# GpSimd's normalised rows ahead of its sums of the chosen in groups 7 and 8, and two uses of PSUM banks 5 and 7 exchanged, in an attention and mixture-of-experts layer

## What is computed

```python
x = x + xattn(layernorm(x), ctx)      # q = xn @ Wq.T; k, v = split(ctx @ Wkv_expand.T)
xf = layernorm(x)                     # softmax(q k / sqrt(32), causal) @ v @ Wout.T
probs = softmax(xf @ gate_w.T); top_p, top_i = top_k(probs, 2)
y = sum of top_p * (silu(xf @ fc1_e) * (xf @ fc2_e)) @ proj_e over the two experts
y = y + sigmoid(xf @ shared_gate_w.T) * ((silu(xf @ s_fc1) * (xf @ s_fc2)) @ s_proj)
x = x + y
```

## Time and profile before

| what | value |
|---|---|
| three runs, median (lowest to highest) | 1514.23 us (1508.57 to 1515.4) |
| the profiled execution: its time, and its span | 1513.03 us, 1511.3 us |
| busy: TensorE, its weight loads | 98%, 83% of the span |
| busy: VectorE, ScalarE, GpSimd | 59%, 43%, 41% |
| mean granted clock of TensorE | 0.99 of full |
| chain that ended last: TensorE, ScalarE, VectorE | 91%, 4%, 2% |

### The profile page before, as it was taken

One profiled execution on the slowest core, in us unless ns is written; L12 is line 12 of the kernel. 1 busy time (PEld: TensorE's weight loads), 2 busy tenths in 40 slices (PEclk: granted clock), 3 DMA queues, 4 the chain that ended last, 5 costly groups with the idle time before them and its releaser, 6 DMA issues.

```text
span 1511.3 us, 28047 instructions
## 1 busy us (share of the span) xinstructions
PE 1477.5 (98%) x9928; PEld 1256.4 (83%) x9928; DVE 894.0 (59%) x1453; ACT 653.0 (43%) x1833; POOL 617.5 (41%) x513
## 2 busy tenths in 40 slices
PE   7999999999789999999999999999999999999999
PEld 7888888887568899999999999887888888888887
DVE  6778888887555587876877867455223232233322
ACT  6999999998653323323323323332112121111211
POOL 3344566666343387685865864102101102011010
PEclk9999999999799999999999999999999999999999
DMA  6243445443155588867877765462303022030210
GB/s 232 80 118 117 124 114 133 125 120 93 52 132 117 155 324 323 270 254 262 284 249 267 267 221 179 167 216 86 97 15 112 28 69 63 8 111 28 64 48 28
DMA packets 102903, 217.42 MB, mean 144 GB/s; under 512 B 43696, under 2 KB 48816, under 8 KB 98064
## 3 DMA queue, kind: packets, MB, share of 16 engines
q1 hardware_dynamic: 91184, 184.71, 37.5%
q0 software_dynamic: 11616, 31.35, 7.1%
HBM read 168.86 MB, written 47.17 MB: 143 GB/s over the span
## 4 chain that ended last, share of the span: by engine, by line
PE 91%; ACT 4%; DVE 2%; DMA 1%; issue 1%; POOL 1%; POOLq 0%; SPq 0%; DVEq 0%; ACTq 0%
PE psum L827 64%; PE psum L1145 11%; PE psum L960 4%; ACT probs L1258 3%; PE psum L951 2%; PE psum L910 2%; PE psum L1047 2%; PE psum L982 2%; PE psum L1071 1%; PE psum L1012 1%; PE psum L969 1%; PE psum L941 1%; ACT probsT L1239 0%; DMA wkv_raw<-in_wkv 0%; POOL xn L1475 0%
## 5 line engine op out<-in xcount | busy, mean ns | idle before, releaser
L1582 POOL DMA_INDIRECT routed<-expert_out_dram,slot_b x56 | 56.8, 1014 | 478.0 <-DVE slot_b L2043 327.5
L2061 DVE TENSOR_TENSOR h_s<-psum,silu_s 128x512 f32<-128x512 f32 x66 | 45.6, 691 | 298.5 <-PE psum L827 298.5
L1258 ACT ACTIVATE probs<-psum,minus_max,rs 112x112 f32<-112x112 f32 x512 | 220.5, 482 | 2.2 <-DVE minus_max L1713 2.0
L827 PE MATMUL psum<-nT_hi,ws_hi 128*128 128x512 f32 x528 | 208.8, 395 | 3.1 <-DVE nT_lo L1984 2.8
L827 PE MATMUL psum<-nT_lo,ws_hi 128*128 128x512 f32 x528 | 208.6, 395 | 0.0
L827 PE MATMUL psum<-nT_hi,ws_lo 128*128 128x512 f32 x528 | 208.6, 395 | 0.0
L1554 POOL DMA_INDIRECT xg<-normed_dram,tile_ids x63 | 150.4, 2388 | 35.7 <-DMA tile_ids<-lists_dram 12.8
L827 PE MATMUL psum<-wj_hi,gT_hi 128*128 128x352 f32 x504 | 162.8, 323 | 0.0
L827 PE MATMUL psum<-wj_hi,gT_lo 128*128 128x352 f32 x504 | 162.3, 322 | 0.0
L827 PE MATMUL psum<-wj_lo,gT_hi 128*128 128x352 f32 x504 | 161.8, 321 | 0.0
L1372 ACT ACTIVATE silu_s<-psum 128x512 f32<-128x512 f32 x66 | 39.5, 598 | 241.3 <-PE psum L827 241.3
(11 more groups left out here) (252 smaller groups left out, 3534.2 us busy)
## 6 DMA issues: line engine op xcount, KB each, us to landing
wj_raw<-in_w_experts SPq DMA_DIRECT2D x35, 1408.0 KB, 6.6
wj_raw<-in_w_experts SPq DMA_DIRECT2D x35, 768.0 KB, 5.9
wj_raw<-in_w_shared SPq DMA_DIRECT2D x22, 768.0 KB, 5.8
expert_out_dram<-y_c SPq DMA_DIRECT2D x63, 256.0 KB, 3.2
base<-x_dram SPq DMA_DIRECT2D x8, 1024.0 KB, 5.8
xT_raw<-in_xT SPq DMA_DIRECT2D x32, 224.0 KB, 4.7
x_in<-in_x SPq DMA_DIRECT2D x32, 224.0 KB, 4.3
x_res<-in_x SPq DMA_DIRECT2D x32, 224.0 KB, 3.0
```

Source lines behind the costliest of these rows:

```text
L827: mm = pe.matmul(out_ap, u, v, start=(n == 0), stop=(n == last))
L1258: done = act.activation(probs[:, j % 2, 4 * r + m, :], psum[0:SEQ, r, m * SEQ:(m + 1) * SEQ], ACT.Exp, bias=minus_max[:, r, m:m + 1], scal ...
L1582: pool.indirect_dma_start(out=routed[:, b % 2, c, :], out_offset=None, in_=expert_out_dram, in_offset=bass.IndirectOffsetOnAxis(ap=slot_b[ ...
L2061: dve.tensor_tensor(h_s[:, :], bank(b), silu_s[:, :], ALU.mult).then_inc(emptied_b[b], 1)
```

## The change

Two parts. In GpSimd's loop `rows(t - 3)` is moved ahead of `sum_chosen(g - 1)`. Both run in one step only in (7, 2), for batch 27, and in (8, 2), for batch 31. In `TURNS` the rows' transposes (`normT`, groups 0 to 7) take bank 7 and the outputs (`outT`) bank 5. At the start of `hidden0` the wait on bank 5's last shares becomes one on bank 7's. No instruction is added or removed.

```diff
@@ TURNS
     TURNS += [((_j, "probsT", k), 1, (7, 5, 4, 6)[k]) for k in range(4)]
-    TURNS += [((_j, "normT", 0), "norm", 5), ((_j, "outT", 0), 1, 7),
+    TURNS += [((_j, "normT", 0), "norm", 7), ((_j, "outT", 0), 1, 5),
               *([((_j, "rank", 0), "rank", 7)] if _j == 2 else []),
@@ TensorE, hidden0
                     pe.wait_ge(S["n0_split"], KC)
-                    wait_emptied(pe, NG, 0, "probsT", 1)
+                    wait_emptied(pe, NG, 0, "probsT", 0)
                     wait_emptied(pe, NG, 0, "outT")
@@ GpSimd, body
+                    if there(g, j, 3) and t - 3 >= FROM:
+                        rows(t - 3)
                     if j == 2 and routes(g):
                         sum_chosen(g - 1)
-                    if there(g, j, 3) and t - 3 >= FROM:
-                        rows(t - 3)
```

## The result

| | median (lowest to highest), runs | profiled execution: span |
|---|---|---|
| before | 1510.79 us (1508.57 to 1515.4), 5 | 1511.3 us |
| after | 1501.68 us (1499.46 to 1502.69), 5 | 1499.9 us |

The ratio is 0.993, with a 95% interval of 0.9912 to 0.9947: the change makes the kernel about 9 us faster (0.7%). The forecast was 1505.9 us, its range ended at 1501.8.

A forecast was written before the change was run, and what follows sets the result against it. TensorE was taken to bound the kernel, busy 90% or more of nearly every slice. Terms -9.25 - 0.5 + 2.0 = -7.75 us, from a base of 1513.6, gave 1505.9 us; range 1501.8 to 1510.2.

The forecast's parts named there:

- Rows ahead of the sums, step 7.2: Group 7, j = 2: TensorE's 6.93 us wait for batch 27's rows goes and the clock recovers; gain 9.25 us.
- The sums are not late: Step 7.2: sums behind the rows still run at 394.5 to 396.25, before `ranks` needs them; cost nothing.
- Step 8.2: Group 8, j = 2: batch 31's rows, ready 0.48 us after TensorE asks, come early; gain 0.5 us.
- Bank 7 for the rows' transposes: Rows' transposes wait for ScalarE's first copy of shares instead of the second; gain 0.
- Bank 5 for the outputs: Queries now wait for VectorE's `aT_lo`, late at j = 0 of groups 3 to 6; 2.0 us lost.
- The collision: Step 7.2: GpSimd's rows pass overlaps VectorE's second multiplication of shares, making it 0.47 us longer; TensorE loses nothing.
- The rivals: Four alternatives: queries never wait (0.16), another wait takes part (0.16), it does not do what it says (0.04), slower (0.04).
- The queries never wait: Rival, chance 0.16: VectorE's lateness in the four steps is made up; -9.75 us, 1503.9 us.
- Slower: Rival, chance 0.04: queries' wait for `aT_lo` spreads from 4 steps to all 27; at 0.75 us each +10.5, 1524.1 us.

The follow-up runs named there:

- the order alone: Only GpSimd's order changed (rows ahead of the sums) against the kernel before, banks as before: 1502.04 us, ratio 0.9932.
- the best of both: Kernel before with GpSimd's new order and the shares' first two quarters exchanged (bank 5, then 7), queries behind the rows' transposes: 1498.69 us, 0.9911.
- the square: Times of 25 steps: before 306.00 us; shares' first two quarters exchanged 302.53; `normT`/`outT` banks exchanged 305.41; both exchanges 307.86.

## Why the prediction was right or wrong

- **Rows ahead of the sums, step 7.2: right.** -9.25 us predicted, -9.66 measured in this pair of executions and -9.0 on the mean of ten traces. The idle time alone (6.93) would have missed 2 to 2.7 us. They came back with the clock, as I said: TensorE's stretch from the rows' transposes to `x1` took 2.84 us less. "All three steps are set by ScalarE's exponentials" was wrong for 7.2 before, which was set by the slow projection and by VectorE behind it. That the measure was good to 0.4 us is in part luck, as a step there takes 11.9 or 13.1 us by the clock of the execution. The predicted length, 13 to 13.5 us, was reached by the order alone (13.15) and the best of both (13.01); the other three have 12.62 to 12.84. The granted clock was to be above 0.8: it is 0.87 from 388 to 401 us after.
- **The sums are not late: right.** They end at 394.33, 2 us before the ranks ask.
- **Step 8.2: right.** -0.5 us predicted. The wait went, and from the rows' transposes of 8.1 to those of 8.2 it is 9.55 us after and 10.18 before, 0.63 less. That the whole rest of the span also came out at -0.5 us says little: it takes between 1085.4 and 1087.9 us in the ten traces.
- **Bank 7 for the rows' transposes: the step that failed.** "In rows 3 they follow the shares' transposes without a gap, so there is nothing to gain: 0." They gained 0.17 us in each of some 25 steps, 2.5 to 3.5 us in all. The chain and the matmul row have no gap because the shares' last matmuls were still draining; the gap was in the weight loads. The term had no bound either: an earlier release was priced at exactly nothing. With it the exchange of banks gained 0.6 to 1.0 us where it was to lose 2.0.
- **Bank 5 for the outputs: right in mechanism, and in its sum by luck.** 2.0 us predicted as four waits of 0.5. Measured were three waits that cost 0.3 each (0.9 us) and two stops of 1.5 us together that I had not seen coming; 1.9 to 2.9 us by the square. A wait of 0.15 us cost 0.3. The upper bound had added "some 0.2 us to start again", which no row before showed; 0.15 is what the runs show.
- **The collision: right.** GpSimd's rows started 0.17 us before VectorE's multiplication, which is the order in which a lock would bite. The timeline of VectorE after:

```profile
386.91 1.53 DVE L1700 TENSOR_TENSOR probs<-probs,rinv 112x896 f32<-112x896 f32 x1
```

  1.09 us became 1.53, as in the earlier trace rows, and TensorE waited 0.26 us for it ("loses nothing" was 0.26 us short). Had it stood until the rows were ready (388.82), it would have ended no earlier than 389.9; it ended at 388.44. The Trainium skill (SBUF — State Buffer, Who interferes with whom) has the two instructions exclude each other from start to end. This trace doesn't bear that out: VectorE's started and ended within GpSimd's, and was stretched by 0.44 us.
- **The rivals.** None of the four was what happened. "The queries never wait" gave a time nearer to the measured one (1503.9), but for the wrong reason: they waited, and the gain came from another place. "Slower" didn't come: the waits for `aT_lo` stayed three, and didn't spread.
- **The sum.** -7.75 us predicted, -9.1 by the medians, -11.4 by the spans of the two profiled executions, of which that of before was 2 us above its median. The base was also high: 1513.6 us was taken, and with two more runs the median of before is 1510.79. Of the 4.2 us between forecast and measurement, 1.4 us are the gain, sized too small, and 2.8 us the base. Against the 1512.08 and 1512.57 of the later sessions the base would be only 1.0 to 1.5 us high, so about half of the 2.8 is scatter of the five.
- **The range.** Its ends don't follow from its own working. 1513.6 less the largest gain (9.6 + 0.5) less 2 us is 1501.5, and 1513.6 less the smallest (6.9 - 2.8) plus 2 us is 1511.5; "1501.8 to 1510.2" is narrower at both ends. The 1501.68 us measured lie between 1501.5 and 1501.8. With the bank term at -0.6 to -1.0 in place of +2.0 the forecast would have been about 1503.

## What to carry to other kernels

To price an earlier release on TensorE, read the idle time in the rows of its weight loads: a wait of 0.2 us there doesn't show in the matmul row or in the chain, and in a loop it counts every time. When two users exchange buffers, ask of each what it now stands behind and who stands behind it now; here one side gained 2.5 to 3.5 us and the other lost 2 to 3, and a table that gave only the first was 2.5 us faster than the change over 25 steps. Where an in-order engine makes something early and something late, put the work whose input is there first: the wait itself cost 6.9 us and the slow clock behind it 2 to 2.8 more. And compare a step in several traces before you believe a microsecond of it.

## What the hardware showed that I had not expected

- A semaphore that comes 0.2 us late for TensorE's load costs 0.17 us, though the matmuls run on without a gap (0.20 us of idle loads, 1.75 against 1.58 us from start to start).
- A shown wait of 0.15 to 0.17 us between two groups of matmuls delayed the second by 0.3 us (1.03 against 0.71 us from the router to the queries). A delay of 0.14 us showed no wait at all (0.85 against 0.71).
- In four kernels with `outT` in bank 5 TensorE stops for 0.5 to 1.1 us in the last quarter of the outputs of steps 1.1 or 3.0, with no releaser in the waits. In all six cases it starts again 1.22 to 1.37 us after the end of a 16 KB "instruction" packet of queue q8 that came some 8 us later than in the kernels without the stop.
- Step 7.3, the same work in ten kernels, took 11.87 to 11.90 us in four executions and 12.99 to 13.14 in six. Its 16 transposes took 1.75 us in the four and 2.89 to 3.24 in the six.
- VectorE's product of two SBUF tiles went from 1.09 to 1.53 us under a GpSimd pass of 2.08 us that had begun 0.17 us earlier. GpSimd's pass was not stretched.
